# Attention scores of a gated cross-attention layer: from six bf16 terms per head to three fp32r terms, two heads in the two halves of the rows

## The reference, cut to what matters

```python
q = split_heads(layernorm(x) @ Wq.T + bq)      # (4, 16, 512, 16)
k = split_heads(ctx @ Wk.T + bk)
v = split_heads(ctx @ Wv.T + bv)
attn = softmax(einsum('bhqd,bhkd->bhqk', q, k) / sqrt(16), axis=-1)
x = x + tanh(g_xattn) * (merge(einsum('bhqk,bhkd->bhqd', attn, v)) @ Wo.T + bo)
x = x + tanh(g_ffn) * ffn(layernorm(x))        # 8 experts, 2 per token, and a shared block
```

## Time and profile before

| | us |
|---|---|
| median of 3 runs | 469.4 |
| lowest and highest | 468.83, 470.41 |
| span of the profiled execution | 466.8 |
| TensorE matmuls busy | 453.6 (97%) |
| VectorE busy | 331.8 (71%) |
| ScalarE busy | 252.6 (54%) |
| POOL busy | 154.4 (33%) |

### The profile page before, as it was taken

How to read it: one execution, slowest core, us unless ns; L and a number is a source line. 1 busy time by engine, 2 the same in 40 slices (tenths; PEclk the granted TensorE clock), 3 DMA queues, 4 the chain that set the end, 5 groups by cost and what they waited for, 6 DMA issues and landing times.

```text
span 466.8 us, 8100 instructions
## 1 busy us (share of the span) xinstructions
PE 453.6 (97%) x2310; PEld 215.8 (46%) x2310; DVE 331.8 (71%) x841; ACT 252.6 (54%) x540; POOL 154.4 (33%) x209
## 2 busy tenths in 40 slices
PE   8999999999999999999999989889999999999997
PEld 8664432222222222222465634565555555555745
DVE  1988898888888888888578766354565656532674
ACT  2664477777777777777565111023666766631110
POOL 5493488111212121212132766600323332332000
PEclk9999999999999999999999999979999999999999
DMA  8669762335353535353548522311322222312921
GB/s 261 223 181 251 157 204 58 86 83 97 90 98 94 98 94 97 95 92 102 167 135 264 211 91 81 110 48 46 93 84 88 85 88 83 90 49 60 377 101 47
DMA packets 54140, 56.71 MB, mean 121 GB/s; under 512 B 13456, under 2 KB 44560, under 8 KB 54096
## 3 DMA queue, kind: packets, MB, share of 16 engines
q1 hardware_dynamic: 47504, 43.82, 34.1%
q0 software_dynamic: 4960, 10.53, 7.4%
q10 hardware_dynamic: 1632, 1.84, 1.2%
HBM read 36.35 MB, written 17.72 MB: 116 GB/s over the span
## 4 chain that ended last, share of the span: by engine, by line
PE 90%; DVE 4%; issue 2%; DMA 1%; SPq 1%; another core or an unknown queue 1%; POOL 1%; ACT 1%; DVEq 0%; POOLq 0%
PE PS L1395 13%; PE PS L1305 13%; PE PS L1523 12%; PE PS L1567 11%; PE PS L1677 9%; PE PS L1580 6%; PE PS L1696 5%; PE PS L1357 4%; PE PS L1672 3%; PE PS L1442 3%; PE PS L1691 2%; PE PS L1651 2%; DVE nmax L842 2%; PE PS L1335 2%; PE PS L1659 2%
## 5 line engine op out<-in xcount | busy, mean ns | idle before, releaser
L842 DVE TENSOR_REDUCE nmax<-PS 128x1 f32<-128x512 f32 x256 | 159.4, 683 | 21.4 <-PE PS L1305 21.4
L730 ACT ACTIVATE R<-PS 128x512 f32<-128x512 f32 x256 | 134.1, 601 | 42.0 <-PE PS L1523 41.7
L1305 PE MATMUL PS<-R 96*128 96x512 bf16 x256 | 96.1, 382 | 1.2 <-DMA R<-k_parts 1.0
L1523 PE MATMUL PS<-R 98*128 98x512 bf16 x256 | 86.2, 380 | 0.3 <-DVE R L860 0.3
L1395 PE MATMUL PS<-R 128*32 128x512 f32 x512 | 68.2, 604 | 0.0
L621 POOL DMA_INDIRECT token_y<-R,dest x34 | 32.6, 960 | 93.4 <-DVE R L1184 92.0
L1305 PEld LDWEIGHTS PS<-R 96*128 96x128 bf16 x256 | 24.8, 97 | 69.7 <-DVE nmax L842 51.1
L1677 PE MATMUL PS<-R 128*128 x100 | 47.3, 595 | 0.2 <-ACT R L798 0.2
L745 ACT ACTIVATE R<-PS 128x512 f32<-128x512 f32 x16 | 9.6, 597 | 68.7 <-PE PS L1567 52.1
L600 POOL DMA_DIRECT2D CH<-R x56 | 27.4, 496 | 54.4 <-ACT R L718 54.4
L1523 PEld LDWEIGHTS PS<-R 98*128 98x128 bf16 x256 | 24.8, 97 | 38.6 <-ACT R L730 22.6
(11 more groups left out here) (177 smaller groups left out, 598.4 us busy)
## 6 DMA issues: line engine op xcount, KB each, us to landing
R<-q_parts SPq DMA_DIRECT2D x96, 64.0 KB, 3.1
R<-k_parts SPq DMA_DIRECT2D x96, 64.0 KB, 3.1
R<-in_fc_w_dram SPq DMA_DIRECT2D x16, 256.0 KB
R<-token_y SPq DMA_DIRECT2D x4, 1024.0 KB, 9.0
R<-slot_x SPq DMA_DIRECT2D x25, 129.0 KB
k_parts<-R SPq DMA_DIRECT2D x8, 384.0 KB, 3.3
q_parts<-R SPq DMA_DIRECT2D x8, 384.0 KB, 3.5
fc<-in_fc_w_dram SPq DMA_DIRECT2D x16, 128.0 KB
```

The source lines that it names most:

```text
L730: nc.scalar.activation(PT[:, kt, j, :], PS[:, (G * (TB * i + kt) + j) % 3, :], ACT.Exp).then_inc(exp_done, 1)
L842: nc.vector.tensor_reduce(nmax[:, i % 2, j * TB + qt:j * TB + qt + 1], PS[:, smax_bank(n), :], AX.X, ALU.max, negate=True).then_inc(max_re ...
L1305: mm(PS[:, smax_bank(n), :], QS[g][0:KS, j, qt * P:(qt + 1) * P], KST[g][0:KS, j, :], start=True, stop=True).then_inc(smax_done, 1)
L1523: mm(PS[:, n % 3, :], KST[g][0:KM, j, kt * P:(kt + 1) * P], QS[g][0:KM, j, :], start=True, stop=True).then_inc(st_done, 1)
```

## The change

It concerns four things.

1. q and k are split into two parts instead of three, the first rounded to fp32r (a reduced 32-bit float), the second the difference. There are three terms instead of six: 48 rows, 50 with the maxima. `second_part` on ScalarE and `third_part` on POOL go.
2. Heads 0 and 2 of a group lie in partitions 0 to 63, heads 1 and 3 in 64 to 127 (`HALF`). A matmul for one head uses one half of the array's rows. `st_done` and `smax_done` become two semaphores each, one for each half.
3. The maxima products go in pairs of heads into two neighbouring banks of 4 to 7, and one VectorE instruction (`two_max`) reduces both. `split_max` on VectorE splits the maxima before the transpose; the transposed pair takes a turn in the three score banks, and one ScalarE copy (`max_rows`) takes it out. The values' sum moves to bank 3, `bias_row` and its product move ahead of the loop.
4. The order on TensorE: the first pair of maxima products stands behind the second score, and behind the values the second pair comes ahead of the fourth score.

The core of the diff (context lines are mostly left out):

```diff
-    TERMS = 6
-    Q_PART = [0, 1, 2, 0, 1, 0]
-    K_PART = [0, 0, 0, 1, 1, 2]
+    TERMS = 3
+    Q_PART = [0, 1, 0]
+    K_PART = [0, 0, 1]
+    UNIT = 2 * TERMS
+    HALF = P // 2
...
-        REST = R3[:, 0:2048].rearrange("p (j n) -> p j n", j=4)
-        QP = R3[:, 5120:8192].bitcast(BF16).rearrange("p (j a n) -> p j a n", j=4, a=3)
...
-        QS = [R1[:, 1024 * g:1024 * (g + 1)].bitcast(BF16).rearrange("p (h n) -> p h n", h=G) for g in range(NG)]
-        KST = [R1[:, 4096 + 1024 * g:4096 + 1024 * (g + 1)].bitcast(BF16).rearrange("p (h n) -> p h n", h=G)
-               for g in range(NG)]
+        QP = R3[:, 4096:8192].rearrange("p (j a n) -> p j a n", j=4, a=2)
...
+        QS = [QK[:, 1024 * g:1024 * (g + 1)].rearrange("p (h n) -> p h n", h=2) for g in range(NG)]
+        KST = [QK[:, 4096 + 1024 * g:4096 + 1024 * (g + 1)].rearrange("p (h n) -> p h n", h=2) for g in range(NG)]
...
-        mparts = sb("mparts", [G * TB, 2, 2, P], BF16)
+        nmax_parts = sb("nmax_parts", [P, 2, 2, G * TB])
+        mparts = sb("mparts", [2 * G * TB, 2, P])
...
+        def max_tile(n):
...
+            i, m = divmod(n, G * TB)
+            h, m = divmod(m, 2 * TB)
+            qt, r = m // 2, m % 2
+            return i, (h, r, qt), 2 * TB * r + TB * h + qt
...
+        def maxima(tiles):
...
+            return min(tiles, EARLY) + max(tiles - EARLY, 0) // 2
...
+        MT_AT = 2 * G + 3
...
+        def score_turn(i, kt, j):
...
+            return (G * TB + 1) * i + G * kt + j + (i + 1 < GROUPS and G * kt + j >= MT_AT)
...
+        def max_turn(i):
...
+            return (G * TB + 1) * (i - 1) + MT_AT
...
         def smax_schedule(i, kt):
...
-        OUT_AT = TB + 1
-        M2_AT = 2 * TB + 1
...
-            return (6, 4, 5)[n % 3] if n < EARLY else 3 + n % 3
+            return (6, 4, 5)[n % 3] if n < EARLY else 4 + (n - EARLY) % 4
...
         def max_user(n):
...
-            return users[-1] + 1 if users else 0
+            return maxima(users[-1] + 1 if users[-1] < EARLY else users[-1] + 2 - users[-1] % 2) if users else 0
...
-            def load_group(i, terms=range(TERMS)):
+            def load_group(i, pieces=range(UNIT)):
...
-                    sp.wait_ge(st_done, G * TB * (i - NG + 1))
+                    for r in range(2):
+                        sp.wait_ge(st_done[r], G // 2 * TB * (i - NG + 1))
+                else:
+                    sp.wait_ge(kones, g + 1)
...
-                for t in terms:
-                    sp.dma_start(QS[g][t * DK:(t + 1) * DK, :, :],
-                                 q_scr[b, Q_PART[t], rows, :].rearrange("(h d) n -> d h n", h=G)).then_inc(ld_group[g], 16)
-                    sp.dma_start(KST[g][t * DK:(t + 1) * DK, :, :],
-                                 k_scr[b, K_PART[t], rows, :].rearrange("(h d) n -> d h n", h=G)).then_inc(ld_group[g], 16)
+                for piece in pieces:
+                    t, r = divmod(piece, 2)
+                    at = slice(HALF * r + t * DK, HALF * r + (t + 1) * DK)
+                    sp.dma_start(QS[g][at, :, :].bitcast(F32),
+                                 q_scr[b, Q_PART[t], rows, :].rearrange("(h r d) n -> r d h n", r=2, d=DK)[r])\
+                      .then_inc(ld_group[g], 16)
+                    sp.dma_start(KST[g][at, :, :].bitcast(F32),
+                                 k_scr[b, K_PART[t], rows, :].rearrange("(h r d) n -> r d h n", r=2, d=DK)[r])\
+                      .then_inc(ld_group[g], 16)
...
             def load_max(i):
-                for part, s in ((0, m1_ready), (1, m2_ready)):
-                    sp.wait_ge(s, i + 1)
-                    sp.dma_start(QS[i % NG][KS + part:KS + part + 1, :, :].rearrange("p h n -> p (h n)"),
-                                 mparts[:, i % 2, part, :]).then_inc(m_in[i % 2], 16)
+                sp.wait_ge(m_ready, i + 1)
+                for part in range(2):
+                    sp.dma_start(QS[i % NG][KS + part:P:HALF, :, :].bitcast(F32).rearrange("p h n -> p (h n)"),
+                                 mparts[G * TB * part:G * TB * (part + 1), i % 2, :]).then_inc(m_in[i % 2], 16)
...
-            def third_part(b, j):
-                pool.wait_ge(q2_ready, 4 * b + j + 1)
-                nc.gpsimd.tensor_tensor(QP[:, j, 2, :], REST[:, j, :], QP[:, j, 1, :], ALU.subtract).then_inc(q3_ready, 1)
...
+            for g in range(NG):
+                nc.gpsimd.memset(KST[g][:, :, :].bitcast(F32), 1.0).then_inc(kones, 1)
+                if g == 1:
+                    rstd_first(2)
+            rstd_first(3)
+            pool.wait_ge(kones, NG)
+            pool.wait_ge(w_in["small"], 64)
+            for c in range(DC):
+                nc.gpsimd.tensor_scalar(bv_wide[:, c, :], ones[:, :], bv_col[:, c:c + 1], None, ALU.mult).then_inc(bv_ready, 1)
+            pool.wait_ge(bv_ready, DC)
+            pool.wait_ge(scaled, 3)
+            nc.gpsimd.tensor_scalar(tg_bo[:, :], bo_row[:, :], tg[:, 0:1], None, ALU.mult).then_inc(bo_scaled, 1)
+            pool.wait_ge(bo_scaled, 1)
...
-                nc.scalar.activation(QP[:, j, 0, :], PS[:, qk_bank(b, j), :], ACT.Identity, bias=bias_of(j),
-                                     scale=1.0).then_inc(q1_ready, 1)
...
-            def second_part(b, j):
-                act.wait_ge(rest_ready, 4 * b + j + 1)
-                nc.scalar.copy(QP[:, j, 1, :], REST[:, j, :]).then_inc(q2_ready, 1)
...
-            def m_first(i):
+                nc.scalar.activation(QP[:, j, 0, :].bitcast(F32R), PS[:, qk_bank(b, j), :], ACT.Identity, bias=bias_of(j),
+                                     scale=1.0).then_inc(high_ready, 1)
...
+            def max_rows(i):
...
-                nc.scalar.copy(mparts[:, i % 2, 0, :], PS[0:G * TB, 7, 0:P]).then_inc(m1_ready, 1)
+                nc.scalar.copy(mparts[:, i % 2, :], PS[0:2 * G * TB, max_turn(i) % 3 if i else 7, 0:P]).then_inc(m_ready, 1)
...
-                        act.wait_ge(st_done, G * (TB * i + kt) + j + 1)
+                        act.wait_ge(st_done[j % 2], G // 2 * (TB * i + kt) + j // 2 + 1)
...
-                        nc.scalar.activation(PT[:, kt, j, :], PS[:, (G * (TB * i + kt) + j) % 3, :], ACT.Exp).then_inc(exp_done, 1)
+                        nc.scalar.activation(PT[:, kt, j, :], PS[:, score_turn(i, kt, j) % 3, :], ACT.Exp).then_inc(exp_done, 1)
...
-                        if j == 1 and kt == 2 and i + 1 < GROUPS:
-                            m_first(i + 1)
+                        if G * kt + j + 1 == MT_AT and i + 1 < GROUPS:
+                            max_rows(i + 1)
...
-            def m_second(i):
-                dve.wait_ge(m1_ready, i + 1)
-                nc.vector.tensor_tensor(mparts[:, i % 2, 1, :], PS[0:G * TB, 7, 0:P], mparts[:, i % 2, 0, :],
-                                        ALU.subtract).then_inc(m2_ready, 1)
+            def two_max(n):
...
+                i, _, at = max_tile(n)
+                for r in range(2):
+                    dve.wait_ge(smax_done[r], n // 2 + 1)
+                nc.vector.tensor_reduce(nmax[:, i % 2, at:G * TB:G * TB // 2], PS[:, smax_bank(n):smax_bank(n) + 2, :], AX.X,
+                                        ALU.max, negate=True).then_inc(max_ready, 1)
...
+            def split_max(i):
...
+                dve.wait_ge(max_ready, maxima(G * TB * (i + 1)))
+                if i >= 2:
+                    dve.wait_ge(mt_done, i - 1)
+                nc.vector.tensor_copy(nmax_parts[:, i % 2, 0, :].bitcast(F32R), nmax[:, i % 2, :]).then_inc(high_max, 1)
+                dve.wait_ge(high_max, i + 1)
+                nc.vector.tensor_tensor(nmax_parts[:, i % 2, 1, :], nmax[:, i % 2, :], nmax_parts[:, i % 2, 0, :],
+                                        ALU.subtract).then_inc(split_ready, 1)
...
             def rest(b, j):
-                dve.wait_ge(q1_ready, 4 * b + j + 1)
-                if b:
-                    dve.wait_ge(q3_ready, 4 * (b - 1) + j + 1)
-                nc.vector.scalar_tensor_tensor(out=REST[:, j, :], in0=PS[:, qk_bank(b, j), :],
+                dve.wait_ge(high_ready, 4 * b + j + 1)
+                nc.vector.scalar_tensor_tensor(out=QP[:, j, 1, :], in0=PS[:, qk_bank(b, j), :],
...
-                                               op0=ALU.add, op1=ALU.subtract).then_inc(rest_ready, 1)
+                                               op0=ALU.add, op1=ALU.subtract).then_inc(low_ready, 1)
...
-                    if b == B - 1 and j == 2:
-                        m_second(0)
+                    if b == B - 1 and j == 1:
+                        split_max(0)
...
-            def head_max(s):
-                for qt in range(TB):
-                    one_max(TB * s + qt)
...
                 normalise(b, B, lambda t: CH[:, b * TB + t, 0:D], h2_ready)
             dve.wait_ge(consts, 9)
+            bias_row()
             for i in range(GROUPS):
                 for kt in range(TB):
-                    s = smax_schedule(i, kt)
-                    if i == 0 and kt == 1:
```

(79 more changed lines are left out.)

79 lines of the change are left out of this document (27 added, 52 removed).

## The result

Changed kernel: 487.23 us median (487.09 at the least). Before, in the same series: 469.12 us (467.0 to 470.41, 4 runs). The ratio is 1.0394, 95% interval 1.0358 to 1.0430: slower by 3.9%, where 462.4 us and a gain were forecast. Ratios and intervals go by the fast runs alone, medians by all runs of a kernel; of the changed kernel's four runs one was slow (516.57 us at a mean granted clock of 0.907). The profiled execution took 487.23 us with a span of 485.5, 18.7 us more than before, at a mean granted clock of 0.979 (before 0.993).

A forecast was written before the change was run, and what follows sets the result against it. TensorE was taken to bound the loop at 2.84 us a step, then a 2.60 us loop of waits. Loop -5.7 and -1.3 before it gave -7.0: span 459.8, median 462.4 us, range 454 to 477.

The forecast's parts named there:

- fp32r takes one pass: Score and maxima products: an fp32r product was taken to cost one pass like bf16, 0.218 us, rather than two or four.
- The loop through the fourth exponential: Attention step: third score, values, maxima pair, fourth score and its exponential form a loop of 2.60 us that becomes the limit.
- The transpose step: Step kt = 2 of each group: the max transpose waits for VectorE's reduction and split, adding 0.70 us a group.
- the bank's turn of the transpose: The max transpose takes a score bank, so the fourth score waits for the second exponential, said to be long done.
- signs of being wrong: fp32r successor in the same half after more than 0.22 us, a pair's products 0.2 apart, or VectorE never waiting.
- weight loads: Loads behind a wait: up to 0.1 us might be laid bare; 0 was taken, 0.1 a step kept for the range.
- first rival: Halves don't overlap: TensorE needs 2.84 us a step again, a group 12.06, time 475 to 478 us; chance 0.16.
- I keep 1.00: TensorE's granted clock in the loop stays at 1.00, since waits of 0.4 us showed no lower clock.
- Before the loop: Ahead of the loop: load wait -0.98 us, first exponential -0.9, early pairs net +0.6; sum -1.3.
- Under TensorE's work: Before the loop: stores growing from 384 to 512 KB were said to be hidden under TensorE's work.
- After the maxima: From 228 us: the first pair saves 0.218 us, two new mode changes cost about as much, so 0.
- 2.6 us between span and median: Median of 469.4 us lay 2.6 above the profiled span of 466.8; carried over to turn 459.8 into 462.4.

The follow-up runs named there:

- the early split: Changed kernel with maxima products one quad further ahead (28 early ones instead of 24), so the maxima split comes a step before the transpose: 479.25 us, ratio 1.0209.
- 128 rows: Changed kernel with every score and maxima product reading rows 0 to 127, so none overlap: 487.10 us (ratio 1.059), on another chip 485.22 (1.054).
- the run with short loads: Changed kernel with two bf16 parts of each operand instead of two fp32r parts, DMAs at half the bytes: 470.39 us, ratio 1.006.

## Why the prediction was wrong

**What held.** fp32r takes one pass, and the halves overlap: the two products of a pair start within 0.01 us of each other, as was said, behind the values too. Reductions of two heads last 1.22 us (forecast 1.13 to 1.2), VectorE does not bound. The loop through the fourth exponential is the limit, with the terms that were named, and it is 2.61 us where its loads are short. The transpose step adds 0.71 (forecast 0.70), with the wait for VectorE ahead of it; that the two agree is in part luck, since with steps of 2.61 us it adds 0.83, where the bank's exponential ends last. The prediction named the bank's turn of the transpose, but gave it no wait of its own.

One of its own signs of being wrong came true: in one half an fp32r product follows the last after 0.24 us, not 0.22. That is only 0.02, and the other two signs did not come.

**The step that failed: weight loads.** "Where a load follows a wait, up to 0.1 us may be laid bare. I take 0 ... and keep 0.1 for the range." The runs show 0.12 at each of two places a step, 0.24. With short loads a group is 11.27, with fp32r loads 12.09, where 11.10 was forecast: 0.82 are the loads, 0.17 the wait at the transpose. The reason given for 0 was the values' product, which starts with its load. But there the start in the timeline is that of the load too; what counts is the time to the result. Behind a wait that was 0.39 us with bf16 loads of 95 ns and 0.50 with fp32r loads of 190: the difference of the loads, to 0.02. The 196 ns of an f32 load stood in the earlier trace rows. The place behind the values was not counted at all: a change of mode lays the next load bare as a wait does (154.52 to 154.86 above). The Trainium skill, TensorE: Matmul & The Clock Gate, Part 2 under LDWEIGHTS, lets a load depend on its columns and not on its rows; its formula gives 107 ns for 128 columns. The traces agree on the rows (190 ns with 50, 188 with 128) and not on the figure for this type.

A group could give away only 0.41 us, 0.10 a step, by the first rival's own sum; this condition was met by loads instead of by halves that don't overlap. (That rival's 475 for half of the mode changes is a slip: 469.4 + 7.7 - 1.9 + 1.5 is 476.7.)

**Clock: "I keep 1.00."** The first two groups took 5.7 us more, of which 1.2 is the longer group. The other 4.5 come in part with the granted clock of 0.50 from 66 to 76 us; the chain of the kernel after has the values there at twice their time:

```profile
67.94 1.86 PE PS L1418 x8
```

The second group is 1.46 longer than the later ones, and its rows at half clock give just that (transpose 0.40 for 0.28, values 1.86 for 1.00, pair 0.72 for 0.43, fourth score 0.43 for 0.24). In the first group VectorE sat idle for 1.74 us ahead of its last reduction (at 70.67), waiting for slow products: at most that much is the clock's. The split behind it took 0.36 and 0.66 us instead of 0.18 twice, 0.66 more, beside a busy POOL; the subtraction took 0.66 and 0.65 in the runs with the early split and with 128 rows too, at a clock of 1.00. The rest of the 4.5, at least 0.6, is not accounted for.

The argument was that only waits of over a microsecond go with a lower clock. Waits do come ahead of this fall: TensorE was busy 5.30 of 6 us from 60 to 66 us, before 5.54. But they are no full account: with the early split it was busy 5.21 of 6 us there and kept 1.00 up to 100 us, and with 128 rows 5.56 and kept 1.00. Nor is it the type: with bf16 in the halves the clock fell as well (0.61 from 66 to 70 us). What sets off the fall at this place stays open.

**Before the loop: -1.3 forecast, +2.6 measured to the first transpose.** The chain of waits of the kernel after:

```profile
23.68 3.54 DMA q_parts<-R
...
32.84 3.96 DMA QK<-k_parts
...
36.84 0.49 PE PS L1320 x2
37.34 1.91 PE PS L1380 x4
```

and TensorE on its timeline, up to the first transpose:

```profile
53.81 1.98 PE L1380 MATMUL PS<-R,w_k 128*128 128x512 f32 x4
56.20 0.28 PE L1337 MATMUL PS<-ident,nmax_parts 128*32 128x128 f32 x1 [0.41 <-DVE nmax_parts L875]
```

"The chain to the first loads shortens by about 2.9 us ... which covers the 0.98": the store is issued 1.8 us earlier (23.68 for 25.46), but it lasts 3.54 instead of 2.58 with 512 KB instead of 384, and the last load 3.96 instead of 3.42. The first maxima product starts at 36.84, before at 36.95, still behind a wait for the load. "Under TensorE's work" was said of the larger stores; they were on the path. From there to the last chunk ahead of the transpose TensorE takes 2.0 us more (36.84 to 53.81, before 36.95 to 51.91): each chunk behind a pair takes 1.91 us instead of 1.72 (the bare load of 0.19 behind a mode change; with products of 128 rows it is 1.72 again), an early pair still takes 0.43, as two products one after the other did, and a single early product 0.42 instead of 0.22. So a pair costs 0.19 more than before, where 0.02 was forecast, and a single one 0.39 instead of 0.24. That last chunk adds another 0.2. Then TensorE waits 0.41 us for the split, which stands behind the last reduction and a rest (L880) on VectorE; the prediction counted this wait inside the loop and left it out here. The first exponential starts at 63.36 instead of 61.06, 2.3 later.

**After the maxima: 0 forecast, 1.9 measured.** Eight products of the output projection (L1465) take 1.92 where they follow a score, before 1.73, and the score behind the values takes 0.43 instead of 0.32: loads laid bare at each change of mode again, 0.3 in each of five steps at the most. Up to the values at 269.74 (before 251.45) that makes 1.5 us; the other 0.4 lies behind them and is not traced to a cause.

**The sum.** The forecast was -7.0 us. To this come, over the 14 groups that it counted, the loads 14 x 0.82 = 11.5, the longer wait at the transpose 14 x 0.17 = 2.4, VectorE's casts beside POOL 1.0 and the clock in the second group 1.5; then the first group 3.6 (clock, split and a rest not accounted for, as above), the stretch before the first transpose 3.9 (1.3 that did not come and 2.6) and the end 1.9. Together that is 18.8, the measured difference of the spans to 0.1. The loads are the largest term, but not the whole of the turn: the run with short loads took back 16.9 of the 18.7 us and was still at a ratio of 1.006, no gain. Of the forecast's 2.6 us between span and median only part was that: in every run listed for the changed kernel the time is 1.7 us above its own span.

## What to carry to other kernels

Price a weight load at its full length wherever its product follows a wait or a change of the tiling, and read the time to the result, not to the start. When an engine stops being the limit because a loop of waits takes over, work out how much that loop can give away before it is as long as before. Here it was 0.10 us a step with the transpose counted, and two loads took 0.24. Before halving the rows of a product, look at the granted clock over the whole run, and compare kernels on one chip.

## What the runs showed that was not expected

- Serial products of 48 and 50 rows had a granted clock of 0.50 for the whole loop with TensorE busy in 50 of 50 us; serial products of 128 rows had 1.00. Two chips, same result: 638 and 629 us against 487 and 485.
- A cast of 128x16 on VectorE lasts 0.77 us instead of 0.18 beside a POOL multiplication of 128x512 (two of 13 groups, 1.0 us in all), and with the early split, which moved it elsewhere, 0.17 or 0.18 in each of them. The Trainium skill, GPSIMD Engine Reference, section Specifications, says that GpSimd shares its SBUF interfaces with VectorE and contends with those of its instructions that have two SBUF inputs or run in a 2-port mode. The trace agrees for the subtraction L875, which has two inputs from SBUF (1.12 us beside the multiplication in one group of the run with the fourth score first, mostly 0.18); whether the cast ran in such a mode no row shows.
- The same kernel, the one before, takes 469.4 us on one chip and 459.8 on another. Its clock of 0.989 to 0.996 against 0.996 to 1.000 accounts for part. For the changed kernel the traces show where: on both chips a group is 12.09 us, but the part behind the last transpose takes 240.8 us on one and 230.1 on the other. The cause is open.
